# A selective scan whose steps hold 64 channels for two state values

## What is computed

```python
xr, z = split(u @ W_in)                    # 192 channels each
x = silu(causal_conv(xr, 4 taps) + b)
dt, Bm, Cm = split(x @ W_x)                # 6, 16 and 16 columns
delta = softplus(dt @ W_dt + b_dt)
def step(h, inp):                          # h: (batch, 192, 16)
    dA = exp(d_t[..., None] * A)           # A = -exp(A_log)
    h = dA * h + (d_t * x_t)[..., None] * B_t[:, None, :]
    y = einsum('bdn,bn->bd', h, C_t)       # sum over n = 0..15
y = (ys + x * D) * silu(z) @ W_out         # L0: then layer norm
```

## Time and profile before

| what | us |
|---|---|
| median of 3 runs | 2221.36 (2218.45 to 2224.84) |
| the profiled execution | 2221.17 |
| its span (first to last instruction) | 2219.4 |
| busy PE / DVE / POOL / ACT | 1823.8 / 1958.8 / 1957.2 / 1136.3 |
| first scan starts / last scan ends | 64.07 / 2191.18 |

### The profile page before, as it was taken

How to read it: one execution, slowest core, us unless ns; L and a number is a source line. 1 busy time by engine, 2 the same in 40 slices (tenths; PEclk the granted TensorE clock), 3 DMA queues, 4 the chain that set the end, 5 groups by cost and what they waited for, 6 DMA issues and landing times. The chain is left out here.

```text
span 2219.4 us, 16413 instructions
## 1 busy us (share of the span) xinstructions
PE 1823.8 (82%) x4490; PEld 698.3 (31%) x4490; DVE 1958.8 (88%) x1276; ACT 1136.3 (51%) x1316; POOL 1957.2 (88%) x856
## 2 busy tenths in 40 slices
PE   5597889798798799789879779879878888876777
PEld 2232233233233333233333223323323333222322
DVE  2898898778998998998999898999889899899995
ACT  3657464645745644644655544644575564453331
POOL 0897988797998997998999899799899989899995
PEclk9798899899999899999999999999999999999898
DMA  3465556436556656664655665565655665566673
GB/s 83 170 206 147 173 176 176 139 130 222 157 189 213 175 170 204 175 197 172 206 156 197 217 176 199 190 162 190 207 155 173 202 191 185 192 205 184 219 218 81
DMA packets 119592, 398.24 MB, mean 179 GB/s; under 512 B 17788, under 2 KB 22156, under 8 KB 119500
## 3 DMA queue, kind: packets, MB, share of 16 engines
q1 hardware_dynamic: 119500, 397.20, 57.7%
HBM read 386.70 MB, written 6.29 MB: 177 GB/s over the span
## 5 line engine op out<-in xcount | busy, mean ns | idle before, releaser
L898 POOL TENSOR_TENSOR ring<-ring,c_ring 128x1024 f32<-128x1024 f32 x576 | 1348.4, 2367 | 113.7 <-DVE ring L835 110.6
L495 PE MATMUL y_ps<-ring,wp 128*128 128x512 f32 x2304 | 1183.8, 627 | 53.0 <-DVE yv_rows L815 28.2
L835 DVE TENSOR_TENSOR_SCAN ring<-a_ring,b_ps 128x1024 f32<-128x1024 f32 x424 | 968.2, 2284 | 28.5 <-ACT a_ring L616 0.3
L495 PEld LDWEIGHTS y_ps<-ring,wp 128*128 128x128 f32 x2304 | 449.9, 199 | 525.0 <-issue 409.6
L801 DVE TENSOR_TENSOR b_ps<-u_ab,b_ps 128x1024 f32<-128x1024 f32 x256 | 310.2, 1212 | 95.6 <-PE b_ps L487 69.2
L616 ACT ACTIVATE a_ring<-delta_ab,neg_a 128x1024 f32<-128x1024 f32 x256 | 290.6, 1142 | 199.2 <-DVE ring L835 194.0
L835 DVE TENSOR_TENSOR_SCAN ring<-b_ps,b_ring 128x1024 f32<-128x1024 f32 x152 | 344.6, 2273 | 27.7 <-ACT b_ps L616 12.3
L892 POOL TENSOR_TENSOR b_ring<-u_ab,b_ring 128x1024 f32<-128x1024 f32 x128 | 306.6, 2396 | 59.2 <-DMA b_ring<-b_rows 59.1
L616 ACT ACTIVATE a_ring<-delta_m,neg_a 128x1024 f32<-128x1024 f32 x168 | 192.3, 1145 | 238.8 <-DVE ring L835 238.7
L487 PE MATMUL b_ps<-b_in,sel 96*128 96x512 bf16 x512 | 164.2, 404 | 102.1 <-DVE ring L835 101.4
L801 DVE TENSOR_TENSOR b_ps<-u_m,b_ps 128x1024 f32<-128x1024 f32 x168 | 203.0, 1209 | 19.6 <-PE b_ps L487 19.6
(11 more groups left out here) (91 smaller groups left out, 1262.0 us busy)
## 6 DMA issues: line engine op xcount, KB each, us to landing
c_ring<-c_rows SPq DMA_DIRECT2D x384, 512.0 KB, 4.8
c_ring<-c_rows SPq DMA_DIRECT2D x384, 256.0 KB, 4.1
b_ring<-b_rows SPq DMA_DIRECT2D x128, 512.0 KB, 4.8
b_ring<-b_rows SPq DMA_DIRECT2D x48, 256.0 KB, 5.2
out<-io SPq DMA_DIRECT2D x16, 192.0 KB, 2.4
io<-x SPq DMA_DIRECT2D x6, 384.0 KB, 4.9
b_in<-parts SPq DMA_DIRECT2D x36, 64.0 KB, 2.0
dt_in<-parts SPq DMA_DIRECT2D x72, 24.0 KB
```

Of the source, the lines that this page charges most:

```text
L495: nc.tensor.matmul(half(y_ps[:, :], j), ident, half(ring[:, g % RING, :], j), start=(n == 0), stop=(n == NS - 1)).then_inc(g_summed, 1)
L835: nc.vector.tensor_tensor_scan(out=h, data0=a, data1=b, initial=0.0, op0=ALU.mult, op1=ALU.add).then_inc(h_ready, 1)
L898: nc.gpsimd.tensor_tensor(r, r, c_ring[:, g % C_RING, :], ALU.mult).then_inc(g_ready, 1)
```

## The change

A step now holds 64 channels for two values of n: partitions 0 to 63 carry n = 2m, partitions 64 to 127 the same channels for n = 2m + 1. Two steps, g even and g + 1, hold two blocks of 64 channels of one batch (phases 0 and 1), or the last block of either batch (phase 2). There are still 16 steps in a phase and 48 in an item.

- Sums: for each pair of steps and each half of 512 times, two matmuls of 64 columns, with two identities stacked in the weights (`stack`), write partitions 0 to 63 and 64 to 127 of `y_ps`. One such pair of matmuls runs in each step, where two of 128 columns did. `SUM_LAG` is 3, but a sum waits for both products of its pair.
- C rows: in phases 0 and 1 one load (two DMAs, to 64 partitions each) serves two steps. `c_ring` has three buffers for four. `load_rows` issues them by a list worked out ahead (`loads`).
- delta and u are made in `delta_in` and `u_in` (128 channels), and a new job `two` has SP copy each block of 64 channels to both halves of the partitions, 8 DMAs of 256 KB in each phase.
- `x_out` and `parts3` hold one half; `bc_in` runs twice, with 11 DMAs each (22 for 13).
- `BY_POOL` has 140 steps for 152 (FWD 10 for 13). The tables are new; the softplus and `u` of phase 2 move to steps 3 to 8 of the item itself (numbered 51 to 56), its `two` to step 16 (64), that of phase 0 to step 32 of the item before and that of phase 1 to step 0.

```diff
-C_RING = 4
+C_RING = 3
-BY_POOL = {ROWS: (2, 8, 13, 17, 19, 23, 26, 30, 31, 37, 47),
-           FWD: (3, 7, 9, 11, 13, 15, 16, 17, 20, 25, 27, 31, 42),
-           BWD: (5, 7, 10, 11, 15, 16, 19, 21, 23, 27, 31, 33, 41, 43)}
+BY_POOL = {ROWS: (4, 13, 18, 19, 23, 26, 30, 31, 37, 42, 47), FWD: (3, 8, 13, 15, 16, 19, 21, 25, 28, 39),
+           BWD: (1, 5, 8, 13, 15, 19, 21, 23, 27, 31, 33, 39, 41, 45)}
...
-PE_ORDER = ("ahead", "sum_0", "jobs", "sum_1")
+PE_ORDER = ("ahead", "sum", "jobs")
-SP_ORDER = ("ahead_b", "ahead_c", "jobs")
+SP_ORDER = ("loads", "jobs")
-SUM_LAG = 4
+SUM_LAG = 3
+TAKE_AT = 4
...
-PREP = dict(xr=(0, 2, 4, 6, 8, 10), skip=(14, 16, 16), dbl=(13, 16),
-            dt=(22, 23, 34, 34, 27, 26), exp=(26, 38, 31), ln=(30, 39, 33), u=(31, 42, 34),
+PREP = dict(xr=(0, 2, 4, 6, 8, 10), skip=(14, 16, 16), dbl=(13, 18),
+            dt=(23, 24, 34, 35, 51, 52), exp=(25, 36, 53), ln=(26, 37, 54), u=(27, 39, 56), two=(32, 48, 64),
...
+        loads = [[] for _ in range(ALL_STEPS)]
+            if g == 0 or c_load[g] != c_load[g - 1]:
+                old = c_load[g] - C_RING
+                loads[max(opens, g - C_LEAD, c_last[old] + 2 if old >= 0 else 0)].append(("c", g))
+            if by_pool[g]:
+                old = pool_before[g] - B_RING
+                loads[max(opens, g - B_LEAD, pool_steps[old] + 1 if old >= 0 else 0)].append(("b", g))
...
+                elif name == "two":
+                    q = phase_of(kind, pair, i)
+                    wait(sp, h_ready, NS * (q - 1))
+                    sp.wait_ge(K["set_ready"][kind], 3 * pair + nth(i))
+                    for src, dst in ((delta_in, delta), (u_in, u_two)):
+                        for sub in range(2):
+                            for e in range(2):
+                                sp.dma_start(dst[e * DM:(e + 1) * DM, q % 2, sub, :],
+                                             src[sub * DM:(sub + 1) * DM, :]).then_inc(two_loaded[q % 2], 16)
...
+            def load_rows(s):
+                for row, g in loads[s]:
+                    kind, pair = step_at(g)[0:2]
+                    sp.wait_ge(c_kept, 64 * (g // STEPS + 1))
+                    if row == "c":
+                        if c_load[g] >= C_RING:
+                            sp.wait_ge(g_ready, c_last[c_load[g] - C_RING] + 1)
...
-                nc.tensor.matmul(half(y_ps[:, :], j), ident, half(ring[:, g % RING, :], j),
-                                 start=(n == 0), stop=(n == NS - 1)).then_inc(g_summed, 1)
+                pe.wait_ge(g_ready, 2 * pair_of + 2)
+                for sub in range(2):
+                    last = nc.tensor.matmul(half(y_ps[sub * DM:(sub + 1) * DM, :], j), stack,
+                                            half(ring[:, (2 * pair_of + sub) % RING, :], j),
+                                            start=(n == 0), stop=(n == NS - 2))
+                last.then_inc(g_summed, 1)
+            def sum_at(s):
+                t = s - SUM_LAG
+                if t > 0:
+                    sum_half((t - 1) // 2, 0 if t % 2 else 1)
```

More of the change, by code:

```diff
@@ L49 @@
         _at += _n
-for _name, _n in [("ident", P), ("mean", C), ("centre", C), ("sel", 2 * NS), ("split", 2), ("ln", 4)]:
+for _name, _n in [("stack", DM), ("mean", C), ("centre", C), ("sel", 2 * NS), ("split", 2), ("ln", 4)]:
     _cols[_name, None] = (_at, _n)
@@ L91, in fills_prep @@
     for j in range(2):
-        for n, name in enumerate(("dbl", "split_hi", "split_mid", "split_lo")):
-            out.append((at["dbl"][j] + n, name, j))
-    out.append((at["dbl"][1] + 4, "bc_in", 0))
+        for n, name in enumerate(("dbl", "split_hi", "split_mid", "split_lo", "bc_in")):
+            out.append((at["dbl"][j] + min(n, 3), name, j))
     for u in range(6):
@@ L100, in fills_prep @@
         out.append((at["u"][k], "u", k))
+        out.append((at["two"][k], "two", k))
     if kind != BWD:
@@ L197, in plan @@
         parts.append(item(FWD, p - 1, *fills))
-        parts.append(item(BWD, p - 1, fills_prep(ROWS, p + 1) if p + 1 < PAIRS else fills_prep(FWD, p)))
-    parts.append(item(FWD, PAIRS - 1, fills_post(BWD, PAIRS - 2), fills_prep(BWD, PAIRS - 1)))
-    parts.append(item(BWD, PAIRS - 1))
+        prep = fills_prep(ROWS, p + 1) if p + 1 < PAIRS else fills_prep(FWD, p)
+        parts.append(item(BWD, p - 1, late, own(prep)))
+        late = spill(prep)
+    prep = fills_prep(BWD, PAIRS - 1)
+    parts.append(item(FWD, PAIRS - 1, late, fills_post(BWD, PAIRS - 2), own(prep)))
+    parts.append(item(BWD, PAIRS - 1, spill(prep)))
     parts.append(alone(fills_post(BWD, PAIRS - 1)))
@@ L421, in job @@
[L421 to L428 removed]
+                    slot, n = parity(kind, pair), ordinal[kind, pair]
@@ new lines, in job @@
+                    landed(sp, "dbl", kind, pair, i)
+                    for g in range(3):
+                        sp.dma_start(half(b_in[B_ROWS * g:B_ROWS * (g + 1), slot, :], i),
+                                     parts3[0:B_ROWS, g, :]).then_inc(K["bc_loaded"][kind], 16)
+                    for q, (g, _) in enumerate(DT_TERMS):
+                        sp.dma_start(half(dt_in[2 * RANK * q:2 * RANK * (q + 1), :], i),
+                                     parts3[B_ROWS:SPLIT_ROWS, g, :]).then_inc(K["dt_loaded"][kind], 16)
+                elif name == "two":
[7 more added lines that the diff above has]
+                                             src[sub * DM:(sub + 1) * DM, :]).then_inc(two_loaded[q % 2], 16)
@@ L553, in job @@
                 if name == "xr_first":
+                    if kind != ROWS and j == 0:
+                        pe.wait_ge(affine_done, 2 * pair + min(k + 1, 2))
                     if i == 0:
```

313 lines of the change are left out of this document (146 added, 167 removed).

## The result

The changed kernel takes 2390.45 us (median of 4 runs, 2389.77 to 2393.15) against 2222.16 for the kernel before: a ratio of 1.0761, 95% interval 1.0742 to 1.078. It is 168 us slower, where 2199 us and a range of 2150 to 2255 had been forecast. The profiled execution has a span of 2391.4 us.

A forecast was written before the change was run, and what follows sets the result against it. PE was taken to bound phase 0, with DVE or POOL busiest or near full in the other phases. From 2221.2 us, -42 (items), +17 (start) and +3 (seam) gave 2199 us, range 2150 to 2255.

The forecast's parts named there:

- Part 1: PE's sums: 1.20 us a step for 1.72, 300 us of PE time; phase 0 of FWD and ROWS shortens.
- later product: Rival, PE's sums: they need the product of step s - 4, delaying B rows; +42 us, 2240; chance 0.09.
- Part 2: DVE and POOL, by phase: moved steps and `u`, plus waits, change four items each by -15, -25 and -2 us.
- the wait in each item: All phases: waits added to the busiest engine's time, such as 2 us in phase 0, 1 for BWD.
- Part 3: DMAs of rows and `two` copies: mostly hidden, 1 us an item taken, between bounds of nothing and 9.
- The rival that copies and loads collide: SP's queue at steps 16 and 32: B and C rows stand behind copies; +56 us, 2254; chance 0.13.
- 20 were the mark: Sign of being wrong: POOL waiting for `c_ring` by DMA for more than 20 us.
- Part 4: Start and seam: `dt` at 60 us, first scan at 82 for 64, +17; between items 1 and 2, +3.
- The seam between items 1 and 2: Between items 1 and 2: scans about 21 us apart for 18.0, so +3.
- the brake everywhere: Rival, PE in all items: 11 items save 82 us, giving 2159; chance 0.25.
- The clock: Rival, PE: with less to do it may get 1.2 GHz more often, losing the gain; 2221; chance 0.07.
- The pairs do run together: Denies a rival on PE's sums: pairs not together, 1.9 us for 1.72, about 2250; chance 0.04.

The follow-up runs named there:

- a_interleaved: Changed kernel with the two values of n on alternating partitions, so a row pair or copy is one transfer to 128 partitions: 2312.88 us, ratio 1.0368.
- the two fixes together: a_interleaved with phase 2's `two` moved behind the first `bc_in`, and two buffers each for `x_out` and `parts3`: 2292.97 us, ratio 1.0312.
- i_tiny_both: a_interleaved with the two fixes together, and its copies of delta and u cut to 16 elements a partition: 2235.94 us, ratio 1.0056.
- b_pair_sums: Kernel before with only its sums done in pairs of 64 columns, layout kept, half the channels left out of the sums: 2197.64 us, ratio 0.9873.
- a_tiny_copies: Changed kernel with each copy of delta and u cut to 16 elements a partition, issues unchanged: 2293.39 us, ratio 1.0327.
- m_transfer_forms: No model computed; six forms of DMA, each alone, against no kernel: three lots at 406 to 423 GB/s, three at 229 to 266.

## Why the prediction was wrong, point by point

By ratios, times 2222 us, the loss of 169 us comes apart in this order: form of the rows (a_interleaved) 87, the two fixes together 12, bytes of the copies (i_tiny_both) 57. Each of the three is uncertain by 7 to 9 us, and the first may hold some of the price of the issues. At 1.0056 there is 12 left over the kernel before, and 41 over b_pair_sums. Of these 41, some 14 are the table, if it costs here what it did there, and 10 the start (first scan at 74.4 for 64.1); some 17 I have not traced. Phase 1 of FWD is still long in i_tiny_both: 64.4, 64.2 and 64.3 us in items 5, 8 and 10, for 59.9, 60.4 and 59.2. In another order the parts are of other sizes (a_tiny_copies took away 96 first), since they do not add.

**Part 1, the sums: right for the instructions, not for where they pay.** PE in the changed kernel, in phase 0 of item 5:

```profile
1059.58 1.99 PE L563 MATMUL bank<-x,w_conv 96*128 96x512 f32 x4
1061.49 1.08 PE L518 MATMUL y_ps<-ring,wp 128*64 128x512 f32 x4
1062.51 1.98 PE L563 MATMUL bank<-x,w_conv 96*128 96x512 f32 x4
```

Four instructions of 64 columns take 1.02 us from start to start, as forecast. The four of 128 columns between two such groups take 1.91 where four alone take 1.72: the switches out and in cost 0.19 together, the two tenths of the earlier trace rows. The drain that the Trainium skill names (TensorEngine Tiling (Array Packing), section Key Properties) is in the trace, and it is small. At the low clock the four of 64 columns show as 1.98 us (at 1121.14) for the 1.08 here. So PE's busy time fell by 181 us in b_pair_sums and by 120 in the change, where 300 had been worked out from rows at full clock. b_pair_sums shows 28 us for the whole kernel, but only 4.6 of them in FWD, where the forecast had 25 of its 42; in phase 0 of item 5 either PE was not what bound it, for all its busy time, or the wait for the pair's later product took the gain back. No run tells these apart.

**Part 2: the busy times right, the waits wrong.** The busier of DVE and POOL in each phase adds to 164.0 (ROWS, item 7), 172.5 (FWD, item 5) and 162.8 (BWD, item 6), where I had 166.0, 170.9 and 165.3. The sums are right with some luck: in FWD about 3 us of DVE's work stood in phase 1 and not in phase 0 (56.8 and 58.5 for the 60.2 and 55.4 forecast). The items last 189.2, 194.1 and 187.5, so they wait 25.2, 21.6 and 24.7 us, where I allowed 6.5, 6.0 and 3.5. The term that was mis-sized is the wait in each item, by 16 to 21 us. From the first scan to the end of the last, the kernel takes 2271.1 us (91.10 to 2362.15) where 2127.1 less 42 plus 3 had been forecast: 183 of the 191 us by which the forecast missed.

**Part 3: the step that failed.** In the sum, the DMAs stood with 1 us an item, since the copies have 16 steps and the bytes fall; the runs give the bytes of the copies 57 us and the form of the rows, with its issues, 87. I costed 2.1 MB of copies at 330 GB/s, 6.3 us, from phase 1 of item 5. That phase had rows to 128 partitions. Phase 2, in the same rows, loads rows to 64 partitions only, and had 146 GB/s at a share of 0.55, 170 at 0.68 and 173 at 0.69: 250 to 265 GB/s for busy engines. That was the nearest row for everything that the change adds, and I took the other. At 235 GB/s (m_transfer_forms) the copies take 9 us, three times an item; and the C and B rows of phases 0 and 1 go to the same poor rate, on which the prediction had no term at all. "Bytes in all fall" was true, and the DMA engines' time rose from 57.7% to 64.8%. The Trainium skill, DMA: Bandwidth & Descriptors, section Where 436 GB/s comes from, gives 435 GB/s, by which I estimated 4.8 us for the copies; transfers over 128 partitions come near it in m_transfer_forms (423 in a slice), those over 64 do not (mostly under 245 GB/s), and there the measurement decides.

**The rival that copies and loads collide** came nearest, at a chance of 0.13 and a price of 56 us. It named the place (steps 16 and 32, 19 issues in a row) and the sign, POOL waiting for `c_ring`, which is 121.6 us where 20 were the mark. Its price was a third of the truth, because it too was made with 6.3 us for a `two`, let it cost once an item, and had no term for the rows' own rate. In the trace a `two` needs 7.5 to 8.2 us to be issued, at the start and at the seam 11.5 and 11.4 until the work that reads it goes on (8.9 in the sum), and three come in each item. A further rival is untested: ScalarE waits 88.8 us, in 17 waits, for copies to land before it may write `u_in` again, which has a single buffer.

**Part 4: too small.** The first scan was to be at 82 and is at 91.1 (from 64.07 that is +27; the +17 of the sum should already have been +18). `dt` starts at 66.6, where 60 was taken and 63 the bound:

```profile
50.27 0.59 ACT L705 ACTIVATE parts<-bank 44x512 bf16<-44x512 f32 x1 [7.62 <-DMA dt_in<-parts]
...
51.49 1.28 DVE L786 CAST sel<-wp 96x1024 bf16<-96x1024 f32 x2
...
58.07 0.18 DVE L815 TENSOR_SCALAR neg_a<-neg_a 128x48 f32<-128x48 f32 x1
58.16 0.68 DVE L902 TENSOR_TENSOR parts<-bank,parts 44x512 bf16<-44x512 f32 x1
...
66.64 1.01 PE L539 MATMUL bank<-dt_in,w_dt_parts 72*128 72x512 bf16 x2 [23.83 <-DMA dt_in<-parts]
```

The first half's `dt_in` are issued by 49.0, the second half's `b_in` only at 58.9. `parts3` was free soon after 49.0, at 50.3. But in DVE's program the constants (L786 to L815), 6.8 us, stand between the two subtractions of the second split (L898 at 50.9 and L902), and they in turn had waited behind L898. In the kernel before they ran after the split, beside the DMAs. The term that was mis-sized is the second split, 3 us in the prediction, nearly 10 in the trace; it left out these constants. From `dt` to the scan it is 24.5 us for the 22 of the sum, by the later landing of the `two`. The seam between items 1 and 2 was too small as well: the last scan before it starts at 448.39 and the next at 473.26, 24.9 us apart for 18.0, so +6.9 where +3 was given.

**The other rivals.** PE was not the brake everywhere: with the sums halved before any other change, the kernel gained 28 us and not 82. The clock did fall, from 0.94 to 0.77; that it costs little is argued from b_pair_sums and i_tiny_both and not measured apart. The pair does wait for its later product: PE waits 131.0 us for POOL's products, 53.9 in b_pair_sums and 1.8 before. DVE's wait for PE did not rise with it, so little of this seems to pass on, but no run takes it out. The pairs do run together.

## What to carry to other kernels

Before counting bytes, divide each window's GB/s by its DMA share: this is the rate of the form of transfer that runs there, and a change that brings more of a form must be costed from a window that has it. A transfer that touches 64 partitions on either side took 1.5 to 1.6 times as long here as one over 128 (lots of 20.7 for 13.9 us and 20.1 for 12.4), so halving the columns of a matmul was bad business here, where it halved the partitions of the transfers that feed it. When a queue is the trouble, a wait that disappears at one engine proves nothing until the next late arrival behind it has been looked for; here each single repair of the order only uncovered the B row. And what stands in an engine's program behind a wait is held with it, as DVE's constants were at the start.
